# A Transformer layer with top-8 experts: the row scatters of a batch spread over one and a half passes of a software-pipelined loop

## The reference

```python
x = x + attention(layernorm(x))          # 16 query heads, 4 key/value heads of 16, rotary, causal
h = layernorm(x)
logits = h @ gate_w.T                    # 64 experts
topv, topi = top_k(logits, 8)            # 8 experts for each token
rw = softmax(topv)
out = sum over the 8 experts e of rw[e] * (silu(h @ gate_e) * (h @ up_e)) @ down_e
out = out + sigmoid(h @ sh_gate1) * shared_expert(h)
x = x + out
```

## Time and profile before

| | |
|---|---|
| median of 3 runs | 1220.87 us (1215.87 to 1222.19) |
| profiled execution | 1212.77 us, its span 1211.0 us |
| mean granted clock of PE | 0.927 of full |
| PE busy | 1023.7 us (85%) |
| DVE, ACT, POOL busy | 59%, 56%, 60% |
| first stage | about 0 to 747 us, a beat takes about 78.5 us |
| second stage | about 751 us to the end |

### The profile page before, as it was taken

One profiled execution on the slowest core, in us unless ns is written; L12 is line 12 of the kernel. 1 busy time (PEld: TensorE's weight loads), 2 busy tenths in 40 slices (PEclk: granted clock), 3 DMA queues, 4 the chain that ended last, 5 costly groups with the idle time before them and its releaser, 6 DMA issues. The chain is left out here.

```text
span 1211.0 us, 24260 instructions
## 1 busy us (share of the span) xinstructions
PE 1023.7 (85%) x7378; PEld 809.7 (67%) x7378; DVE 710.7 (59%) x2229; ACT 676.3 (56%) x1650; POOL 723.8 (60%) x954
## 2 busy tenths in 40 slices
PE   2799989899989898898998611999999999999962
PEld 1466666666666666666665401999989889999950
DVE  2466776767767677777674550222236656666666
ACT  2366665666656656666554101777656667766630
POOL 3111122774856847658367775577777777777770
PEclk9689999999999999999898855999999999999985
DMA  2388876821312313212132994777778989998735
GB/s 89 131 261 278 270 250 209 285 100 44 112 56 80 118 32 110 83 58 97 39 133 81 323 321 155 217 220 219 219 265 313 374 307 339 316 357 282 260 111 187
DMA packets 142157, 233.23 MB, mean 193 GB/s; under 512 B 17271, under 2 KB 119878, under 8 KB 136656
## 3 DMA queue, kind: packets, MB, share of 16 engines
q1 hardware_dynamic: 67216, 101.06, 25.8%
q0 software_dynamic: 27648, 69.28, 15.8%
q10 hardware_dynamic: 47168, 61.35, 15.3%
HBM read 107.32 MB, written 132.66 MB: 198 GB/s over the span
## 5 line engine op out<-in xcount | busy, mean ns | idle before, releaser
L1363 POOL DMA_INDIRECT res_d<-y,dst_i x320 | 321.6, 1005 | 111.0 <-issue 82.8
L453 POOL DMA_INDIRECT rows_d<-pay,slot_i x256 | 258.4, 1009 | 73.4 <-issue 67.8
L858 DVE TENSOR_REDUCE nmax<-ps 128x1 f32<-128x512 f32 (+3 forms) x448 | 225.6, 530 | 103.7 <-PE ps L508 101.8
L724 ACT ACTIVATE wgu_s<-ps 128x512 f32<-128x512 f32 x320 | 191.3, 599 | 108.2 <-PE ps L508 105.0
L508 PE MATMUL ps<-mask,ident_b 128*128 128x256 bf16 (+1 forms) x640 | 172.2, 269 | 0.0
L501 PE MATMUL ps<-kT,qT 96*128 96x512 f32 (+3 forms) x512 | 166.8, 388 | 6.2 <-DVE nmax L858 4.0
L1294 PE MATMUL psB<-wgu_s,xT 128*128 x1280 | 171.9, 278 | 0.0
L1311 PE MATMUL psD<-wdp_s,innerT 128*128 x640 | 165.7, 382 | 3.7 <-ACT innerT L1199 2.5
L548 PE MATMUL ps<-qT,kT 128*128 128x512 f32 (+3 forms) x512 | 161.3, 377 | 0.9 <-ACT qT L737 0.6
L1294 PEld LDWEIGHTS psB<-wgu_s,xT 128*128 128x128 f32 x1280 | 158.2, 195 | 0.4 <-issue 0.4
L1118 DVE TENSOR_TENSOR inner<-inner,psB 128x128 f32<-128x128 f32 x160 | 45.7, 286 | 188.9 <-ACT inner L1193 185.6
(11 more groups left out here) (241 smaller groups left out, 1622.3 us busy)
## 6 DMA issues: line engine op xcount, KB each, us to landing
rows_d<-blank ACTq DMA_DIRECT2D x8, 5440.0 KB, 19.4
xg<-rows_d SPq DMA_DIRECT2D x160, 272.0 KB
yk<-res_d SPq DMA_DIRECT2D x32, 1024.0 KB
wgu_s<-wgu_in ACTq DMA_DIRECT2D x8, 1024.0 KB, 13.5
xs<-x_d SPq DMA_DIRECT2D x32, 192.5 KB
x_d<-x SPq DMA_DIRECT2D x30, 192.5 KB, 2.5
res_d<-y,dst_i POOLq DMA_INDIRECT x320
wgu_s<-x_in SPq DMA_DIRECT2D x32, 128.0 KB, 2.1
```

The source lines that it names most:

```text
L453: pool.indirect_dma_start(rows_d, bass.IndirectOffsetOnAxis(ap=slot_i[par][:, t, k:k + 1], axis=0), pay[par][:, t, :], None).then_inc(s_sc ...
L724: act.activation(pexp[p % 4][:, s, :], ps2[:, (5 * p + s) % 2, :], ACT.Exp, scale=HEAD_D ** -0.5).then_inc(s_exp, 1)
L858: return dve.tensor_reduce(nmax[u][:, tile, heads[0]:heads[-1] + 1], src, AX.X, ALU.max, negate=True)
L1363: pool.indirect_dma_start(res_d, bass.IndirectOffsetOnAxis(ap=dst_i[:, j % (2 * G):j % (2 * G) + 1], axis=0), y[:, j % Y, :], None, bounds ...
```

## The change

Three things change, all in `beat` and only for POOL, which alone has a scatter step.

1. In a beat with main part, scatters stand at the end of their slot, behind route, pre, post and products.
2. In beats 2 to 6 (main, late and pre) only 21 scatters of batch b-2 are issued, one in each of the slots 14 to 38 but 17, 19, 26 and 33 (`SAME_BEAT`). The other 11 follow in the next beat, in slots 0 to 7 and 10 to 12 (`NEXT_BEAT`), as the scatters of `older`, which is batch b-3. So beats 3 to 7 begin with 11 scatters among the route steps.
3. In beat 7 (no pre) the 32 scatters of batch 5 keep their slots, but at the slot's end. Beats 8 and 9 keep slots and place.

```diff
--- before.py
+++ after.py
@@ -201,6 +201,10 @@
             PRE_AT, PRE_EVERY, PRE_PARTS = 0, 9, 11
             POST_AT, POST_EVERY, POST_PARTS = 11, 7, 8
             SCATTER_AT = 13
+
+            SAME_BEAT = [k for k in range(14, SLOTS - 1) if k not in (17, 19, 26, 33)]
+            NEXT_BEAT = [k for k in range(13) if k not in (8, 9)]
+            assert len(SAME_BEAT) + len(NEXT_BEAT) == TILES * TOP
             ROUTE_AT, ROUTE_PARTS = 1, 12
 
             FIRST_EVERY = 5
@@ -255,9 +259,10 @@
                     if late and not routed and 0 <= slot - ROUTE_AT < ROUTE_PARTS:
                         steps["route"](h - 1, par, slot - ROUTE_AT)
                     first, spread = (1, 33) if routed else (SCATTER_AT, SLOTS - SCATTER_AT)
-                    for n in range(TILES * TOP):
-                        if late and slot == first + n * spread // (TILES * TOP):
-                            steps["scatter"](h - 1, par, n)
+                    if routed:
+                        for n in range(TILES * TOP):
+                            if slot == first + n * spread // (TILES * TOP):
+                                steps["scatter"](h - 1, par, n)
                     for t in reversed(range(TILES)):
                         k = slot - PRE_AT - PRE_EVERY * t
                         if pre and -PRE_AT <= k < PRE_PARTS:
@@ -268,6 +273,14 @@
                         if behind and -1 <= k < POST_PARTS:
                             steps["post"](*prv, t, k)
                     steps["products"](*ago, s)
+                    older = (h - 1, 0) if par == 1 else (h - 2, 1)
+                    if main and older[0] >= 0 and slot in NEXT_BEAT:
+                        steps["scatter"](*older, len(SAME_BEAT) + NEXT_BEAT.index(slot))
+                    if main and late and pre and slot in SAME_BEAT:
+                        steps["scatter"](h - 1, par, SAME_BEAT.index(slot))
+                    for n in range(TILES * TOP):
+                        if main and late and not pre and slot == first + n * spread // (TILES * TOP):
+                            steps["scatter"](h - 1, par, n)
```

## The result

| | before | after |
|---|---|---|
| median | 1218.66 us (4 runs, 1215.87 to 1222.19) | 1259.14 us (4 runs, 1257.68 to 1260.68) |
| ratio | | 1.0347, 95% interval 1.0305 to 1.039 |
| profiled execution | 1212.77 us | 1260.68 us |
| mean granted clock of PE | 0.927 | 0.903 |
| PE busy | 1023.7 us, 7378 products | 1050.4 us, 7378 products |

The change costs 40 us. Lines of the changed file stand 13 further down than those of the kernel before (L657 is L670, L664 is L677, L298 is L311, L310 is L323, L453 is L466).

A forecast was written before the change was run, and what follows sets the result against it. PE was taken to bound the attention loop, POOL's queue the stretch before the second stage. 16.8 - 0.5 + 2.8 + 1.0 + 1.3 + 4 for the clock = 25.4 us more, hence 1246 us; range 1228 to 1262.

The forecast's parts named there:

- The sum without the clock: Route-product waits in beats 3 to 6 16.8 us, less 0.5 gained; beat 7 2.8 and 1.0; last POOL stretch 1.3.
- Rival A: PE's later waits in the beat shrink, 2 of 4.2 us return four times: +13, 1234 us; chance 0.13.
- B: Route steps have unseen room at L657 and DVE's gain reaches PE: 14 us faster, 1207 us; chance 0.04.
- D: Route-step stalls only replace PE's later stalls, all 4.2 us comes back: no change, 1221 us; chance 0.05.
- rival C: Scatters held up on POOL, two low-clock stretches a beat: +10 on the forecast, 1256 up to 1268 us; chance 0.12.
- O: Rival raised in the experiments: the new order costs by itself, since beat 2 grew 4.4 us; no chance given.

The follow-up runs named there:

- the two halves: Changed kernel with only the scatters of slots 0 to 2, or only 3 to 5, kept ahead of the route products; ratios 1.0145 and 1.0148 against the kernel before.
- the kernel with seven behind the route steps: Changed kernel with 25 scatters in the same beat and seven in the next, in slots 6 to 11 behind the route steps; 1225.06 us, ratio 1.0023.
- the last experiment: Against the kernel before, scatters put into POOL's free stretches: 28 same beat, 4 next beat, beat 7 in the old order; 1224.09 us, ratio 1.0043.

## Why the prediction was right, and the term that was off

**Right.** Direction and mechanism: the two waits at L657 and L664 (expected 1.9 and 2.3 us, measured 1.55 and 1.6 to 2.2 in beats 3 to 6; counted from the transposes of slot 2, PE comes to the second product 4.75 us later than before in beat 4, where 4.2 was expected), shown by the two halves and by the kernel that moves these six scatters. Beat 7: 0.58 us at L670 and 1.96 at L677, 2.5 together, for the 2.8 expected, though split otherwise. One scatter more behind the last long wait: 1.2 us for 1.3. The waits that the change takes away: DVE's for xb and for the deviations of tiles 2 and 3 are gone, that for the rotation products has stayed, and PE got 0.5 us of it, as written. DVE never waited for `s_scat` in slot 15. The sum without the clock was 16.8 - 0.5 + 2.8 + 1.0 + 1.3 = 21.4 us; the runs give 20.9 and 19.4 once the clock is taken out, and in the profiled execution PE is idle 14.8 us longer in beats 2 to 6, for 16.3 expected. Rival A (part is caught up) did not come about: PE's waits other than the two new ones come to 34.3 us in beats 2 to 6, where they were 34.0. B and D are out.

**The term that was mis-sized is the clock.** The step that failed is the 0.8 us a beat put down for it. The prediction took the 0.02 of granted clock between two beats for what a pair of waits can cost, 0.8 us a beat, 4 us in all, with 12 as the bound. Measured: 48 to 51 us more at half clock, 17 to 19 us by the line, and 28.8 us of longer products between the two profiled executions in beats 2 to 6. In the profile, beats 3 to 6 ran at 0.89 to 0.90 and not at 0.98. The low clock outlasted the second wait by far: from L664 to the transposes of tile 0 in slot 16 PE took 21.6 us in place of 18.4, with 1.2 us of waiting on the way as before. The beats that were to take 83 us took 87 to 91, and the last scatter began at 795 us where it was to end near 772. The total rose by 40 us for the 25 of the sum, and the median came out at 1259, near the upper end of the range, by this term; that the range holds it is owed to the room left for rival C, and not to the sum. Of the two things in rival C, one did not happen: no scatter was held up, 256 of them took 962 ns in the middle and 1315 at most, as before. The other, more low clock in a beat, did, and went further than C had it. The Trainium skill's port rule (SBUF — State Buffer, the box on "DVE blocks DMA"), by which they would have cost 12 us more a beat, is not borne out for them.

**What stays open.** Why a beat falls to half clock without a new wait. Up to slot 13 of beat 2 the changed kernel is the same program as the one before. In the first execution the clock is at 0.50 from 201.8 to 208.6 us, which is ahead of that slot, with PE busy all the time; beat 2 took 83.5 us at 0.92, with no wait for POOL at a route product. In the second execution there is no low clock at that place:

```profile
189.30:267.80 78.50, 71.87 (x548) 51.64 (x549) 56.51 (x172) 49.10 (x114) 39.61 (x67) 0.98 0.57 189
```

Of the 11 traces whose programs are alike up to there, 8 have low clock at this place, just behind the second route product, and 3 have none, the kernel before among them. So the 5 us of beat 2 are chance of the run and not the order's doing, which O had made them. But the changed kernel's eight runs all have 231 us or more at half clock, and only one run in 30 of the kernel before has as much as 227: in beats 3 to 6 it is not chance. Both its executions have a low stretch of 10 us or more at the second wait in each of these beats; without the waits, in the kernel with seven behind the route steps, such stretches are shorter (6.8 us at 358.4 and at 443.7) and missing in one beat of these four. Products in place of part of the waits took back half. What the other half hangs on, the idle time that was left, the lower share of time that PE works in the whole beat or the order of waits and small products, was not told apart.

## What to carry to other kernels

A step that is moved "out of the way" of the steps one watches goes in front of others: list, for the queue it is moved into, every step behind it and who waits there, and compare the room in front of that wait (here 1.4 us at L657) with what is put in (3.7 us of scatters). A wait in a loop that PE bounds can cost twice, once itself and once in the clock behind it, here in roughly equal parts by the line. Where runs carry their granted clock, a line through the runs of one kernel gives an estimate of the two, and PE's busy and idle time over the same products, before and after, gives them for one pair of executions.

## What the runs showed of the hardware

**Half of the loss went with the clock.** With waits of 1.55 and 1.6 to 2.2 us at the two route products, in a loop in which PE is busy nine tenths of the time, the granted clock over the whole beat was 0.89 to 0.91, four beats in a row, in two executions; in the kernel before it was 0.98 to 1.00. That the waits bring part of this is shown by the products put in their place; the whole of it is not.

**A two-input operation of DVE stands still beside POOL's residual, and here and there beside a scatter.** The kernel before has it once a beat and without harm, between the same kinds of operations:

```profile
385.11 0.74 POOL L431 TENSOR_TENSOR xb<-xr,cst 128x256 f32<-128x256 f32 x1
385.13 0.76 DVE L873 TENSOR_TENSOR mt<-nmax,mt 128x8 fp32r<-128x8 f32 x1
```

```profile
L873 DVE TENSOR_TENSOR mt<-nmax,mt x64: 167/168/757, 58.8 to 658.3; 128x8 fp32r<-128x8 f32 x64
```

L873 works on 8 numbers per partition and takes 0.17 us; beside L431 it takes as long as L431 does. The Trainium skill (SBUF — State Buffer, the rule of the shared port pair) says that a DVE operation with two SBUF inputs and a GpSimd operation that reads SBUF exclude one another for the whole of the instruction; these rows agree.

Beside a scatter such an operation mostly keeps its time, but not always. In beats 3 to 5 of the changed kernel the same operation (L886 there) begins 0.47 us behind the start of a scatter, with nothing else on POOL, and takes 0.43 to 0.44 us instead of 0.17. In beat 4:

```profile
371.30 1.09 POOL L466 DMA_INDIRECT rows_d<-pay,slot_i  x1 [0.80 <-POOL col L313]
371.77 0.44 DVE L886 TENSOR_TENSOR mt<-nmax,mt 128x8 fp32r<-128x8 f32 x1
```

In the last experiment L857 took 1297 ns at most and 217 in the middle. The long one begins 0.5 us behind the start of a scatter and 0.47 us ahead of the residual, by when it would long have ended, so the residual alone does not explain it. Why some operations are held beside a scatter and most are not was not told apart.
